# Causal attention: where the diagonal blocks of the two narrower query tiles are masked

## The reference, cut to what matters

```
def _L1_attn_ref(x, Wq, Wk, Wv, Wo, bo, rel_emb):
    b, s, d_in = x.shape                      # 8, 512, 256
    h, hd = (16, d_in // 16)                  # 16 heads of 16
    q = (x @ Wq).reshape(b, s, h, hd).transpose(0, 2, 1, 3)      # k, v likewise
    dist = jnp.clip(jnp.abs(r[None, :] - r[:, None]), 0, 16)
    a_k = rel_emb[dist]
    scores = jnp.einsum('bhqd,bhkd->bhqk', q, k) * a_k
    causal = jnp.triu(jnp.ones((s, s), dtype=bool), k=1)
    scores = jnp.where(causal, -jnp.inf, scores)
    attn = jax.nn.softmax(scores / np.sqrt(hd), axis=-1)
    ctx = jnp.einsum('bhqk,bhkd->bhqd', attn, v)
    return ctx @ Wo + bo
```

## Time and profile before

| | |
|---|---|
| median of 3 runs | 3007.82 us (3002.8 to 3012.21) |
| the profiled execution | 3000.66 us, its span 2998.7 us |
| the attention stage's units | about 2165 to 2690 us of the span |
| PE busy over the span | 2777.9 us (93%) |
| DVE, ACT, POOL busy over the span | 56%, 52%, 44% |

### The profile page before, as it was taken

One profiled execution on the slowest core, in us unless ns is written; L12 is line 12 of the kernel. 1 busy time (PEld: TensorE's weight loads), 2 busy tenths in 40 slices (PEclk: granted clock), 3 DMA queues, 4 the chain that ended last, 5 costly groups with the idle time before them and its releaser, 6 DMA issues. The chain is left out here.

```text
span 2998.7 us, 53882 instructions
## 1 busy us (share of the span) xinstructions
PE 2777.9 (93%) x19171; PEld 1991.6 (66%) x19171; DVE 1685.1 (56%) x4823; ACT 1554.1 (52%) x2621; POOL 1323.3 (44%) x1345
## 2 busy tenths in 40 slices
PE   8899999878999998798999997999789999998999
PEld 6799999733444443477999996666446666655666
DVE  6421221288899998572122113776676666666766
ACT  2233333359999999322333332333277777773332
POOL 6344444379999999263444443200144444320000
PEclk9799999889999999768999998999899999999999
DMA  9399999712222222366999996000333433301000
GB/s 316 108 328 325 329 328 324 220 42 65 66 66 66 66 66 65 99 197 195 321 329 328 324 329 177 1 0 0 88 81 88 100 90 92 75 1 41 14 14 22
DMA packets 307465, 433.58 MB, mean 145 GB/s; under 512 B 29553, under 2 KB 258070, under 8 KB 304150
## 3 DMA queue, kind: packets, MB, share of 16 engines
q1 hardware_dynamic: 281830, 395.64, 42.1%
q0 software_dynamic: 24576, 33.96, 5.2%
q10 hardware_dynamic: 816, 0.79, 0.1%
HBM read 356.99 MB, written 73.33 MB: 144 GB/s over the span
## 5 line engine op out<-in xcount | busy, mean ns | idle before, releaser
L1867 ACT ACTIVATE f_h_t<-f_h_ps,f_b_t 128x128 f32<-128x128 f32 x1024 | 319.4, 363 | 596.7 <-PE f_h_ps L1825 596.7
L2274 POOL TENSOR_TENSOR a_dmg_buf<-a_c 128x2048 f32<-128x2048 f32 x128 | 520.3, 4097 | 44.8 <-PE a_dmg_ps L2340 23.1
L1825 PEld LDWEIGHTS f_h_ps<-f_rows_t,f_w 128*128 128x128 f32 x4096 | 482.3, 194 | 9.9 <-issue 3.5
L1825 PE MATMUL f_h_ps<-f_rows_t,f_w 128*128 128x128 f32 x4096 | 483.4, 277 | 2.3 <-DVE f_rows_t L1881 1.2
L1839 PE MATMUL f_y_ps<-f_w,f_h_t 128*128 128x256 f32 x2048 | 483.4, 379 | 0.0
L1785 POOL DMA_INDIRECT acc_rows<-f_y,f_give x128 | 205.0, 1602 | 487.9 <-DMA acc_rows<-f_y,f_give 450.8
L1839 PEld LDWEIGHTS f_y_ps<-f_w,f_h_t 128*128 128x128 f32 x2048 | 369.8, 190 | 39.9
L1881 DVE COPY f_rows_t<-f_t_ps 128x256 f32<-128x256 f32 x128 | 54.3, 425 | 595.9 <-PE f_t_ps L1813 595.9
L2652 DVE SCALAR_TENSOR_TENSOR a_bond_buf<-a_a,a_small_rep,a_q_ps 128x512 f32<-128x512 f32 x512 | 347.4, 742 | 10.3 <-PE a_bond_ps L2340 5.1
L1043 ACT ACTIVATE a_prob<-a_prob,a_neg_top 128x384 f32<-128x384 f32 (+3 forms) x512 | 276.5, 569 | 39.2 <-POOL a_neg_top L864 38.9
L586 DVE SCALAR_TENSOR_TENSOR x_resid<-f_y_ps,f_gate,x_resid 128x256 f32 (+1 forms) x512 | 217.7, 478 | 130.7 <-PE f_y_ps L422 122.4
(11 more groups left out here) (359 smaller groups left out, 4078.5 us busy)
## 6 DMA issues: line engine op xcount, KB each, us to landing
f_w<-in_L_ffn_w_dram SPq DMA_DIRECT2D x256, 1024.0 KB
a_skewed<-skew SPq DMA_DIRECT2D x32, 512.0 KB, 5.6
a_k_s<-parts SPq DMA_DIRECT2D x16, 768.0 KB, 7.9
acc_rows<-x_resid SPq DMA_DIRECT2D x17, 512.0 KB, 8.1
a_vals<-val_rows SPq DMA_DIRECT2D x64, 136.0 KB, 3.0
xn_rows<-f_xn SPq DMA_DIRECT2D x16, 512.0 KB, 7.4
skew<-a_bond SPq DMA_DIRECT2D x128, 64.0 KB, 1.7
x_resid<-acc_rows SPq DMA_DIRECT2D x30, 256.0 KB, 6.3
```

The source lines that it names most:

```text
L1825: last = nc.tensor.matmul(h_ps[n // HB][:, (n % HB) * P:(n % HB + 1) * P], w1_sb[s][:, c, n * P:(n + 1) * P], rows_t[e % 2][:, c, :], star ...
L1867: nc.scalar.activation(h_t[k][:, n, :], h_ps[n // HB][:, (n % HB) * P:(n % HB + 1) * P], ACT.Gelu, bias=b1_t[:, n, e:e + 1]).then_inc(gelu ...
L2274: nc.gpsimd.tensor_tensor(dmg_buf[n % RING][:, :, :], places(c_sb[h], first_place(dg)), c_sb[h][:, PAD:].unsqueeze(1).broadcast_to([P, DG, ...
```

## The change

For tile 0 and tile 1 (`NARROW`) the mask matmul is gone. DVE multiplies the diagonal block without taking a maximum; for tile 1 the block left of it is multiplied apart, with its maximum, into a new `top_whole`. POOL overwrites what lies above the diagonal with -1e30 by an `affine_select` in place in `prob` (`mask`). DVE then reduces the masked block to its maximum (`find_top`), and POOL's negate takes, for tile 1, the larger of the two maxima. Tiles 2 and 3 keep matmul, multiply and negate. The offsets become `SCORES_AT, TTR_AT, MASK_AT, TOP_AT, NEG_AT, EXP_AT = 8, 6, 5, 4, 3, 2`: on POOL mask(s + 5) stands ahead of negate(s + 3) in each step, on DVE find_top(s + 4) behind multiply(s + 6). The products are placed by the same offsets, so each comes one step earlier relative to the transposes; so do `split_middle` and `split_low`, whose places are relative to `TTR_AT`.

```diff
-    SCORES_AT, TTR_AT, NEG_AT, EXP_AT = 7, 5, 4, 2
+    SCORES_AT, TTR_AT, MASK_AT, TOP_AT, NEG_AT, EXP_AT = 8, 6, 5, 4, 3, 2
+    NARROW = (0, 1)
...
+    def narrow_before(u):
+        return sum(unit(w)[1] in NARROW for w in range(GU)) * (u // GU) + sum(unit(w)[1] in NARROW for w in range(u % GU))
...
             def negate(u):
-                pool.wait_ge(s_taken, UNIT_USE[u] + 1)
+                group, t, g = unit(u)
+                at = slice(u % PR, u % PR + 1)
+                if t in NARROW:
+                    pool.wait_ge(top_ready, narrow_before(u) + 1)
+                else:
+                    pool.wait_ge(s_taken, UNIT_USE[u] + 1)
                 if u >= PR:
                     pool.wait_ge(exp_ready, u - PR + 1)
...
+                if t in NARROW and t:
+                    nc.gpsimd.tensor_scalar(neg_top[:, at], top[:, at], top_whole[:, at], -1.0, ALU.max,
+                                            ALU.mult).then_inc(top_negated, 1)
+                else:
+                    nc.gpsimd.tensor_scalar(neg_top[:, at], top[:, at], -1.0, None, ALU.mult).then_inc(top_negated, 1)
+
+            def mask(u):
+                group, t, g = unit(u)
+                if t in NARROW:
+                    block = prob[:, u % PR, t * P:(t + 1) * P]
+                    pool.wait_ge(s_taken, UNIT_USE[u] + 1)
+                    nc.gpsimd.affine_select(out=block, in_=block, compare_op=ALU.is_ge, fill=MASKED, base=0,
+                                            pattern=[[-1, P]], channel_multiplier=1).then_inc(masked, 1)
...
-                if s + NEG_AT < ALL and s + NEG_AT >= 0:
+                if 0 <= s + MASK_AT < ALL:
+                    mask(s + MASK_AT)
+                if 0 <= s + NEG_AT < ALL:
                     negate(s + NEG_AT)
...
+                last = nc.tensor.matmul(bank[:, 0:width], q_s[half % QK][0:ROWS, h, t * P:(t + 1) * P],
+                                 k_s[half % QK][0:ROWS, h, 0:width], start=True, stop=t in NARROW)
+                if t in NARROW:
+                    last.then_inc(s_ready, 1)
+                else:
+                    nc.tensor.matmul(bank[:, t * P:width], ident_b[:, :], mask_b[:, :], start=False,
+                                     stop=True).then_inc(s_ready, 1)
...
+                if t in NARROW:
+                    if t:
+                        nc.vector.tensor_tensor_reduce(
+                            out=prob[:, u % PR, 0:t * P], in0=s_ps[use % SB][:, 0:t * P], in1=factor[:, S - width:S - P],
+                            scale=1.0, scalar=-3.0e38, op0=ALU.mult, op1=ALU.max,
+                            accum_out=top_whole[:, u % PR:u % PR + 1])
+                    nc.vector.tensor_tensor(prob[:, u % PR, t * P:width], s_ps[use % SB][:, t * P:width], factor[:, S - P:S],
+                                            ALU.mult).then_inc(s_taken, 1)
+                    return
...
+            def find_top(u):
+                group, t, g = unit(u)
+                if t in NARROW:
+                    dve.wait_ge(masked, narrow_before(u) + 1)
+                    nc.vector.tensor_reduce(top[:, u % PR:u % PR + 1], prob[:, u % PR, t * P:(t + 1) * P],
+                                            AX.X, ALU.max).then_inc(top_ready, 1)
...
                 if s + TTR_AT < ALL:
                     multiply(s + TTR_AT)
+                if 0 <= s + TOP_AT < ALL:
+                    find_top(s + TOP_AT)
```

More of the change, by code:

```diff
@@ L751, in attn1_phase @@
         mask_f = prob[:, 5, 0:P]
+        top_whole = sb("top_whole", [P, PR])
         top = sb("top", [P, PR])
@@ L785, in attn1_phase @@
         s_taken = sem("s_taken")
+        masked = sem("masked")
+        top_ready = sem("top_ready")
         top_negated = sem("top_negated")
@@ L860, in negate @@
             def negate(u):
-                pool.wait_ge(s_taken, UNIT_USE[u] + 1)
+                group, t, g = unit(u)
[4 more added lines that the diff above has]
+                    pool.wait_ge(s_taken, UNIT_USE[u] + 1)
                 if u >= PR:
                     pool.wait_ge(exp_ready, u - PR + 1)
-                nc.gpsimd.tensor_scalar(neg_top[:, u % PR:u % PR + 1], top[:, u % PR:u % PR + 1], -1.0, None,
-                                        ALU.mult).then_inc(top_negated, 1)
+                if t in NARROW and t:
[10 more added lines that the diff above has]
+                                            pattern=[[-1, P]], channel_multiplier=1).then_inc(masked, 1)
             nc.gpsimd.memset(mask_f, 0.0).then_inc(mask_made, 1)
```

## The result

The changed kernel takes 3037.77 us, median of 4 (3037.18 to 3041.89), against 3010.02 for the kernel before on the same chip: a ratio of 1.0101, interval 1.0083 to 1.0119. It is slower by 1.0%, 30 us by the ratio. The forecast was 3032 us, +24. The profiled execution took 3037.18 us, its span 3035.3 against 2998.7.

A forecast was written before the change was run, and what follows sets the result against it. PE was taken to set the pace, ACT close behind. Stalls of 37.8 us less 8.6 for masks and 5 credited gave +24 us: 3024.7 us profiled, median 3032; own range 3016 to 3050, 8 in 10 2998 to 3053.

The forecast's parts named there:

- the three points worked out: Scores(21) to turn(18) at q, scores(28) to turn(25) and to turn(27) at k: late transpositions on PE.
- the straight line: DVE's 128-element reduction, priced between 12 elements at 160 ns and 768 at 953: 0.28 us.
- The gross stall of 37.8 us: PE's late transpositions at q and k products: 14 x 1.1 + 14 x 1.6 us, before gains are taken off.
- 1.1 was taken: Stall at each of 14 q products: turn(18) starts at 2393.2 and not 2392.09, +1.1 us.
- took at nothing: Stalls at v and input products: zero to 0.3 us each, taken as zero, with 8 us as far end.
- the 1.6 for k: Stall at each of 14 k products: turn(27) starts at 2404.1 and not 2402.50, +1.6 us.
- half the stalls with the full gain: Low end of the forecast's own range: stalls half as long (19 us), full remaining gain; 3016 us.
- v and input added with nothing caught up: High end of the forecast's own range: v and input add their 8 us, no idle time credited; 3050 us.
- 144 are left: Of 256 removed mask matmuls, 112 lie ahead of stalls and gain nothing; 144 x 0.06 = 8.6 us gained.
- The start-to-start distance: Price of one mask matmul on PE from successive starts: 0.06 us, against its length of 0.221 us.
- The 5 us of idle time credited as caught up: Part of the stalls falls in PE's earlier idle time for ACT's copies (13.5 us); 5 us taken off.
- The second stall at k: PE's late turn(27): negate(28) now stands behind both splits on POOL; +1.6 us, held separate from turn(25)'s stall.

The follow-up runs named there:

- e3_offsets_wait: e2_offsets with negate(u) also waiting for the multiply of unit u + 2 where that is tile 0 or 1, no select or reduction; ratio 1.0043 to the kernel before.
- e4_negate_first: The changed kernel with negate(s + 3) put ahead of mask(s + 5) in POOL's step; 3014.71 us, ratio 1.0034 to the kernel before.
- e2_offsets: The kernel before with offsets 8, 6, 3, 2 for scores, multiply, negate, exponential, mask matmuls kept; ratio 0.9977.
- e11_tile0: The changed kernel with only tile 0 changed; tile 1 gets back its mask matmul and one multiply; ratio 1.0027 to the kernel before.
- e12_tile1: The changed kernel with only tile 1 changed (NARROW = (1,)) and a stricter wait in `normalise`; ratio 1.0074 to the kernel before.
- e1_no_masks: The kernel before with the 256 mask matmuls of tiles 0 and 1 left out and nothing in their place; ratio 0.9988, not told apart from no change.
- e5: The changed kernel with negate(s + 3) ahead of mask(s + 5) and both splits one POOL step later; ratio 1.0044 to the kernel before.
- e9_select_twice: The changed kernel with each select on POOL done twice, the second waiting for the first; 3091.66 us, ratio 1.0281 to the kernel before.

## Why the prediction was right, and where it was off

*The mechanism and its places: right.* The chain from the scores through take, multiply, select, negation, exponential and copy to a late transposition was predicted link by link; at the three points worked out it came within 0.2 us (3.86, 3.96, 6.40 us against 3.83, 3.93, 6.2). e3_offsets_wait shows that the wait alone costs 16.4 us, and e4_negate_first that putting the negation ahead of it gives 19.9 back. The changed kernel stands 38.2 us over e2_offsets. So about half of that is the wait which the wide tiles have no need of; the rest comes with the longer chain itself (select, reduction, longer negation), and how it is shared among these no run shows.

*The added work: right for single instructions.* The reduction takes 280 ns (0.28 predicted by the straight line between the earlier trace rows), the select 295, and no engine's sum became a bound. The two-input negation is longer than taken, 291 against 212 ns. DVE's total was overstated: its busy time rose by 49 us, 6 in a batch element and not 9 to 12. The prediction also lays POOL's select beside DVE's multiply of the same block to say that the one engine is no slower than the other. The select reads one block, the multiply two, one of them in PSUM, and no run here has the select on DVE, so what it would cost there is not shown.

*The sum: +30 measured against +24, near in part by luck.* The gross stall of 37.8 us looks like the 38.2 us that the changed kernel stands over e2_offsets, but it isn't made of the same terms. Laid unit by unit beside e2_offsets (mean of batch elements 2 to 7), e11_tile0 falls back by 1.0 and 0.8 us at the two q products, where 1.1 was taken, and e12_tile1 by 1.8 us at each of the two k products, where 1.6 was taken. e12_tile1 also falls back by 0.7 us at the input product of unit 60 and 0.3 us at the v product of unit 44, which the prediction took at nothing; in the changed kernel PE stands idle 0.57 us for ACT's copy there, ahead of turn(57). These add to more than 38.2 us, and small gains between the sites take the difference back. Part of the 1.6 for k is an addition that comes out too low: from negate(26) at 2400.51 the lengths that the prediction lists lead to 2403.28 and not 2403.1, and so to +1.8. The ends of its own range don't follow from its words either: half the stalls with the full gain give 3018 and not 3016, and v and input added with nothing caught up give 3045 and not 3050.

*The term that failed: the masks.* "144 are left: 144 x 0.06 = 8.6 us gained." All 256 removed gave 5.6 us in the stage, and by the ratio perhaps nothing (e1_no_masks). The start-to-start distance was a better price than the length, but still not one: it is what PE's queue gets back, and waits further on, for ACT's copies and for DVE, took two thirds of it.

*Terms that cancelled.* Moving the products was costed at the shift of the chain only; the new offsets alone gain 5.9 us (e2_offsets). Without this gain, which no term of the sum has, the stage would have lost 38 us and not 32. The 5 us of idle time credited as caught up didn't show as such: PE's idle ahead of transposes rose by 43 us, more than the 25 to 35 named. And the last batch element, which has no products, was to get shorter by 1 to 2 us; it takes 57.3 us against 57.2. Leaving the masks out alone shortens it by 0.6 us (e1_no_masks).

*The second stall at k.* It was put down to both splits standing ahead of negate(28). e5 moved them by a step and gained 0.5 us over six batch elements and nothing by the ratio, because `split_low` then stands ahead of negate(29) and the stall comes a unit later. The price was nearly right and the cause too narrow: it is not one place but what POOL has queued in those steps, and in e2_offsets, with the same splits ahead of negate(28) and no selects, PE stands idle only 0.21 us ahead of turn(27).

## What to carry to other kernels

Where an engine's instructions stand in a fixed order, as POOL's do here, a new instruction can cost more by what is queued behind its wait than by its length: look which producer it waits for, whether that producer is late at some steps, and put the instructions that others wait for ahead of it. Swapping two lines here was worth 20 us, while taking 256 matmuls from the busiest engine was worth 5. Price a removed instruction by leaving it out alone before building the replacement. And cut a stage into its repeating parts before comparing two profiles: the part that holds the noise then shows itself.

## What was not expected of the hardware

The negation on POOL takes 291 ns in its new form against 212 ns in the old one, for the same 128 x 1 output. The new form has a column as second operand and a second operation, and no run tells the two apart.

A stretch at half clock stood behind the longest stalls of PE. In e9_select_twice it came in all six of batch elements 2 to 7, each time behind the second k product, with the granted clock at 0.50 for 6.8 us. In the changed kernel and e12_tile1 it came in one of the six, and in e3_offsets_wait, e4_negate_first and e5, whose stalls are shorter, in none. The DMA engines are at their busiest in the same stretch (share 1.00), and no run keeps the two apart, so the cause is not shown.
